# A decoder layer on one core: head values centred by TensorE, squares taken from PSUM, x2 normalised by ScalarE, the first chunk's attention prepared in the last state-space chunk

## What is computed

```python
# 1. state space: delta = softplus(x W), per step h = exp(delta*A)*h + delta*B*x, y = sum(h*C) + Dp*x, layer norm, W_out
# 2. gated attention, 4 heads of 32 columns, sequence length 64
log_D = log_fg_mat + swapaxes(ig)            # causal, gates in logarithms
D = exp(log_D - max(log_D))
C = (q k^T / sqrt(32)) * D
normalizer = maximum(abs(sum(C)), exp(-max_log_D))
h = (C / (normalizer + 1e-6)) @ v            # q = x, k = v = context
out = (h - mean(h)) * rsqrt(var(h) + 1e-5) * outnorm_scale       # per head
# 3. mixture of 8 experts, the best 2 for each token
```

## Time and profile before

| | us |
|---|---|
| median of 3 runs | 725.03 |
| lowest, highest | 715.24, 731.83 |
| the profiled execution | 720.35 |
| its span, first to last instruction | 718.5 |

### The profile page before, as it was taken

How to read it: one execution, slowest core, us unless ns; L and a number is a source line. 1 busy time by engine, 2 the same in 40 slices (tenths; PEclk the granted TensorE clock), 3 DMA queues, 4 the chain that set the end, 5 groups by cost and what they waited for, 6 DMA issues and landing times.

```text
span 718.5 us, 10709 instructions
## 1 busy us (share of the span) xinstructions
PE 535.5 (75%) x3309; PEld 378.0 (53%) x3309; DVE 447.3 (62%) x975; ACT 308.4 (43%) x628; POOL 373.4 (52%) x318
## 2 busy tenths in 40 slices
PE   3497878889788688777365779787895959999900
PEld 1032424335243335666354668676684748899900
DVE  1589999999999973379657475746361431222245
ACT  2455474856648342122132445454442413333327
POOL 1497978989788754113543354534444342333351
PEclk9999999999999988555556698999797978999955
DMA  5433435344462514463252544442434336689774
GB/s 160 148 120 139 155 133 192 125 165 155 161 189 106 205 61 89 89 99 67 57 139 44 162 150 146 149 170 92 141 126 152 110 132 201 218 284 296 252 227 132
DMA packets 87545, 106.63 MB, mean 148 GB/s; under 512 B 40912, under 2 KB 68816, under 8 KB 87360
## 3 DMA queue, kind: packets, MB, share of 16 engines
q1 hardware_dynamic: 78800, 93.08, 42.1%
q0 software_dynamic: 4320, 8.92, 3.6%
q10 hardware_dynamic: 4368, 3.93, 1.7%
HBM read 93.57 MB, written 12.34 MB: 147 GB/s over the span
## 4 chain that ended last, share of the span: by engine, by line
issue 30%; POOL 19%; PE 18%; DVE 14%; DMA 9%; ACT 4%; SPq 2%; another core or an unknown queue 1%; DVEq 0%; POOLq 0%; ACTq 0%
POOL hc L660 9%; PE pB L1058 6%; DMA wslot<-in_expert_w 5%; DVE h L1477 3%; PE pq L1071 3%; POOL xg_dram L760 3%; PE py L840 3%; POOL y_dram L769 2%; DVE u L1468 2%; ACT x_all L1430 1%; PE py L1058 1%; POOL bcs L613 1%; DMA y_dram<-dx,xin 1%; POOL bc_rest L605 1%; DMA Crep<-c_dram 1%
## 5 line engine op out<-in xcount | busy, mean ns | idle before, releaser
L660 POOL TENSOR_TENSOR hc<-h,Crep 128x1024 f32<-128x1024 f32 x64 | 150.0, 2355 | 23.7 <-DVE h L1477 22.6
L769 POOL DMA_INDIRECT y_dram<-dx,xin x71 | 68.8, 968 | 155.9 <-ACT dx L1354 146.7
L1058 PE MATMUL pB<-Crep,wslot 128*128 128x256 f32 (+1 forms) x556 | 121.7, 365 | 18.7 <-DMA wslot<-in_expert_w 10.3
L840 PE MATMUL py<-hc,ident 128*128 128x512 f32 x256 | 122.8, 608 | 4.3 <-POOL hc L660 4.3
L1058 PEld LDWEIGHTS pB<-Crep,wslot 128*128 128x128 f32 x556 | 92.7, 208 | 36.5 <-DMA wslot<-in_expert_w 13.1
L1468 DVE TENSOR_TENSOR u<-dx,pC 128x1024 f32<-128x1024 f32 x64 | 76.9, 1202 | 18.5 <-PE pC L829 18.5
L840 PEld LDWEIGHTS py<-hc,ident 128*128 128x128 f32 x256 | 49.4, 196 | 55.3 <-issue 42.1
L1791 DVE TENSOR_TENSOR Crep<-u,pB 128x512 f32<-128x512 f32 x35 | 24.0, 686 | 86.9 <-PE pB L1058 48.5
L829 PE MATMUL pC<-bcs,sel 96*128 96x512 bf16 x128 | 41.0, 403 | 45.0 <-DVE u L1468 39.8
L1477 DVE TENSOR_TENSOR_SCAN h<-pa,u 128x1024 f32<-128x1024 f32 x32 | 73.0, 2281 | 0.0
L1477 DVE TENSOR_TENSOR_SCAN h<-pB,u 128x1024 f32<-128x1024 f32 x32 | 73.0, 2281 | 0.0
(11 more groups left out here) (224 smaller groups left out, 948.2 us busy)
## 6 DMA issues: line engine op xcount, KB each, us to landing
wslot<-in_expert_w SPq DMA_DIRECT2D x46, 768.0 KB
Crep<-c_dram SPq DMA_DIRECT2D x64, 512.0 KB, 3.7
h<-m_dram SPq DMA_DIRECT2D x16, 256.0 KB
xin<-xg_dram SPq DMA_DIRECT2D x25, 130.0 KB
xbuf<-in_x_tok SPq DMA_DIRECT2D x8, 256.0 KB, 4.6
cT_st<-in_ctx_T SPq DMA_DIRECT2D x8, 256.0 KB, 4.6
dx<-in_ctx_T SPq DMA_DIRECT2D x8, 256.0 KB, 4.7
delta<-in_ctx_tok SPq DMA_DIRECT2D x32, 64.0 KB
```

The lines of the kernel that those rows point to most:

```text
L660: nc.gpsimd.tensor_tensor(hc[:, K % 4], h[:, K % 3], Crep[:, K % 4].rearrange("p a t -> p (a t)"), ALU.mult).then_inc(hc_done, 1)
L769: nc.gpsimd.indirect_dma_start(out=y2_dram, out_offset=bass.IndirectOffsetOnAxis(ap=xin[:, i % NX, a, D:D + 1].bitcast(i32), axis=0), in_= ...
L840: last = nc.tensor.matmul(py[:], ident[:], hc[:, K % 4, i * CH:(i + 1) * CH], start=False, stop=(K % STEPS == STEPS - 1 and i == 1))
L1058: last = nc.tensor.matmul(bank[:, o * a * P:(o + 1) * a * P], wslot[:, i % NW, stage * F + f * P:stage * F + (f + 1) * P], xgT[i % 2][:, 0 ...
```

## The change

- Values: TensorE multiplies the context by a 128x128 matrix `hcenter` (identity minus 1/32 within each head), so each head's values are centred before they are weighted; ScalarE copies them from PSUM (`copy_values`). The four DMAs for the values go, hsum and the centring too.
- Squares: ScalarE squares the weighted values straight from PSUM; the sum is multiplied twice by the reciprocal of the normaliser. Part 0 multiplies by outnorm out of PSUM; one factor (`vfac`) is applied in part 9.
- Gates: `add_gates` goes; the exponent becomes 16 instructions of 64 columns, each with its gate as bias, after `scale_heads` instead of before it.
- x2: part 13 makes only the shift, ScalarE normalises with four instructions.
- Logits and ranks go to pa[:,1]; `turn_x2` waits for the ranks to be read, `logits` no longer for hv.
- First chunk: its buffers are in wslot's space, so its context, maxima, mask, exponents, values and first scores stand in the last state-space chunk or right behind it; orders are changed on all engines.

```diff
+        lmask = (flatw[:, 0:W2], u[:, 0])
+        mb = (flatw[:, 0:W2], h[:, 2])
...
@@ SyncE @@
-            store_m(0)
             next_rows(NCH - 1)
-            load_m(0)
-            load_heads(0)
-            load_v(0)
+            load_heads(1)
+            load_m(1)
             next_rows(NCH)
-            load_m(1)
...
+                    if c + 1 == NCH and k == 1:
+                        load_heads(0)
+                    if c + 1 == NCH and k == 6:
+                        store_m(0)
+                    if c + 1 == NCH and k == 7:
+                        load_m(0)
...
@@ GpSimd, in the loop over the steps @@
                     weigh_state(STEPS * c + k)
+                    if c + 1 == NCH and k == 6:
+                        start_mask(0)
...
                         if c == 1:
                             mask_constants()
+                            head_constants()
...
@@ TensorE @@
+            def head_values(c):
+                pe.wait_ge(heads_loaded, 16 * (c + 1))
+                pe.wait_ge(ones_set, H + 2)
+                if c:
+                    pe.wait_ge(sq_done, c)
+                else:
+                    pe.wait_ge(u_done, STEPS * NCH)
+                for b in range(TB):
+                    last = nc.tensor.matmul(pC[:, 0, b * P:(b + 1) * P], cTc[late(c)][:, b * P:(b + 1) * P], hcenter[:],
+                                            start=True, stop=True)
+                last.then_inc(values_made, 1)
...
             def turn_x2(c):
                 pe.wait_ge(x2_done, c + 1)
                 if c:
-                    pe.wait_ge(x2T_copied, c)
+                    pe.wait_ge(ranks_read, c)
...
             sum_state(STEPS * NCH - 2)
+            head_values(0)
+            scores(0, 0)
+            scores(0, 1)
             sum_state(STEPS * NCH - 1)
             turn_m(0)
             center_y(NCH - 1)
-            scores(0, 0)
+            scores(0, 2)
+            scores(0, 3)
             variance(NCH - 1)
             turn_x1(NCH - 2)
-            scores(0, 1)
+            weighted_values(0, 0)
+            weighted_values(0, 1)
             project(NCH - 1)
             gate_products(NCH - 2)
-            scores(0, 2)
-            weighted_values(0, 0)
-            scores(0, 3)
-            weighted_values(0, 1)
...
-                expert_units(first[1:3])
+                expert_units(first[1:2])
+                if front:
+                    head_values(c + 1)
+                expert_units(first[2:3])
...
@@ ScalarE @@
             def weight_decay(c):
-                act.wait_ge(log_decay_done, c + 1)
-                if c:
+                act.wait_ge(causal_done, c + 1)
+                act.wait_ge(g_made, 1 if c < GATED[0][1] else 2)
+                if c == 1:
+                    act.wait_ge(hc_done, STEPS * NCH)
+                elif c:
                     act.wait_ge(C_done, c)
-                nc.scalar.activation(Dm, lmask, ACT.Exp).then_inc(D_done, 1)
+                for m in range(TB * H):
+                    last = nc.scalar.activation(Dm[late(c)][:, m * S:(m + 1) * S], lmask[late(c)][:, m * S:(m + 1) * S], ACT.Exp,
+                                                bias=g_sb[:, c * TB * H + m:c * TB * H + m + 1])
+                last.then_inc(D_done, 1)
...
+            def normal_x2(c):
+                act.wait_ge(x2_shift_done, c + 1)
+                act.wait_ge(z2_rstd_done, c + 1)
+                for b in range(TB):
+                    last = nc.scalar.activation(x2_rows(c)[:, b], z2[:, b], ACT.Identity, scale=rstd[:, b:b + 1],
+                                                bias=nma[:, b:b + 1])
+                last.then_inc(x2_done, 1)
...
+            weight_decay(0)
             z_scale(NCH - 2)
             copy_y(NCH - 1)
+            copy_values(0)
             normal_x1(NCH - 2)
             square_y(NCH - 1)
             y_scale(NCH - 1)
             copy_x1T(NCH - 2)
             floor_gates(0)
-            weight_decay(0)
...
+                if mid:
+                    scale_heads(c)
                 if front:
                     weight_decay(c + 1)
-                if mid:
-                    scale_heads(c)
+                    copy_values(c + 1)
                 expert_units(first[2:])
...
                 if mid:
                     z2_scale(c)
+                    normal_x2(c)
                 expert_units(second[2:])
...
@@ VectorE, order of a round @@
-                mid(0)
-                if front:
-                    add_gates(c + 1)
-                mid(1, 2, 3, 4)
+                mid(0, 1, 2)
+                rt(0)
+                mid(3, 4)
                 expert_units(first[0:1])
-                mid(5, 6)
-                rt(0)
+                mid(5, 6, 7)
                 expert_units(first[1:2])
-                mid(7)
                 rt(1)
                 if front:
                     weights(c + 1, 0)
...
-                mid(8)
+                mid(8, 9)
                 rt(7)
+                mid(10)
                 if front:
                     weights(c + 1, 1)
                 expert_units(second[0:1])
                 rt(8)
-                mid(9)
+                mid(11)
                 rt(9)
-                mid(10)
+                mid(12)
                 expert_units(second[1:2])
-                rt(10)
-                mid(11)
-                rt(11)
-                mid(12)
+                rt(10, 11)
+                mid(13)
                 rt(12, 13, 14, 15, 16)
-                expert_units(second[2:3])
-                mid(13)
-                expert_units(second[3:])
+                expert_units(second[2:])
                 rt(17, 18, 19, 20)
...
             row_stats(NCH - 2)
+            log_norm(0)
             row_means(NCH - 2)
-            log_norm(0)
-            add_gates(0)
+            weights(0, 0)
+            weights(0, 1)
             residual_rows(NCH - 1)
-            weights(0, 0)
             keep_gates(NCH - 2)
-            weights(0, 1)
```

More of the change, by code:

```diff
@@ L132, in decoder_layer @@
         norm_inv = sb("norm_inv", [P, TB * H])
-        hsum = sb("hsum", [P, TB * H])
+        vfac = sb("vfac", [P, TB * H])
+        hcenter = sb("hcenter", [P, P])
+        nma = sb("nma", [P, TB])
         vsum = sb("vsum", [P, TB * H])
@@ L374, in decoder_layer, with late @@
         CONSTS = 24
+        def late(c):
+            return int(c >= 1)
         def close_wait(engine):
@@ L467, in next_rows, with store_m, load_m, load_heads @@
                     sp.dma_start(cT_st[:], ctx_T[:, tokens(c - 1)]).then_inc(context_loaded, 16)
+            m_v = m_dram.rearrange("(c n) (j s) -> j c n s", n=TB * H, j=2)
+            def store_m(part):
+                lo, hi = (v * TB * H for v in GATED[part])
+                sp.wait_ge(m_ready, part + 1)
+                sp.dma_start(m_dram[lo:hi], mrow[lo:hi, part]).then_inc(m_stored, 16)
+            def load_m(c):
+                sp.wait_ge(m_stored, 16 * (1 if c < GATED[0][1] else 2))
+                if c == 1:
+                    sp.wait_ge(hc_done, STEPS * NCH)
+                elif c:
+                    sp.wait_ge(causal_done, c)
+                for j in range(2):
+                    sp.dma_start(mb[late(c)].rearrange("p (m s) -> p m s", s=S)[64 * j:64 * j + 64],
+                                 m_v[j, c:c + 1].broadcast_to([64, TB * H, S])).then_inc(maxima_loaded, 16)
+            def load_heads(c):
+                if c == 1:
+                    sp.wait_ge(u_done, STEPS * NCH)
+                elif c:
+                    sp.wait_ge(qk_done, H * c)
+                    sp.wait_ge(values_made, c)
+                sp.dma_start(cTc[late(c)], ctx_T[:, tokens(c)]).then_inc(heads_loaded, 16)
             store_C(0)
@@ L1588, in weights @@
                     pick = lambda v: v.rearrange("p (b h s) -> p h b s", h=H, s=S)[:, hh]
-                    last = nc.vector.scalar_tensor_tensor(pick(Cm), bank, scale, pick(Dm), ALU.mult, ALU.mult)
+                    last = nc.vector.scalar_tensor_tensor(pick(Cm[late(c)]), bank, scale, pick(Dm[late(c)]), ALU.mult, ALU.mult)
                 last.then_inc(C_done if pair else C_half, 1)
@@ L1594, in normalize @@
                 s0 = c * NSTEP
+                heads = hv.rearrange("p (m e) -> p m e", m=M)
+                lines = hv.rearrange("p (b d) -> p b d", b=TB)
                 if part == 0:
                     dve.wait_ge(av_done, c + 1)
+                    if c:
+                        dve.wait_ge(z2_done, c)
+                    else:
+                        dve.wait_ge(hc_done, STEPS * NCH)
+                    for a in range(2):
+                        half = TB // 2
+                        last = nc.vector.tensor_tensor(hv[:, a * half * D:(a + 1) * half * D].rearrange("p (b h e) -> p b h e", b=half, h=H),
+                                                       pav[:, a].rearrange("p (b h) e -> p b h e", h=H)[:, :, :, 0:HD],
```

(4 more changed lines are left out.)

200 lines of the change are left out of this document (87 added, 113 removed).

## The result

The changed kernel takes 746.58 us (median of 5 runs, 746.28 to 751.53) against 725.03 (715.24 to 731.83): 1.0358 times as long, 95% interval 1.0311 to 1.0405, slower. So the two profiles stand 31 us apart and the medians 21.5; what the traces say of places holds, their sum overstates.

What follows compares the result with a forecast made beforehand. VectorE was taken to bound rounds 1 to 3, a loop through GpSimd's sends and the queues the late rounds. Terms 1.5+1.6+10.0+5.4+3 = 21.5 us gave 742 from the profiled execution, 746 from the median; forecast 743, range 735 to 748 (chance 0.5).

Steps and rivals of the forecast that it cites:

- Two of my signs: Signs of being right: rounds 1 and 2 near 20 and 28 us; rounds 5 to 7 unchanged or 1 to 3 longer.
- Round 0: From chunk 0's first normalising instruction to chunk 1's: exponents again behind the heads' scale, +1.6 us.
- Sixteen exponents: ScalarE's exponent as sixteen 64-column instructions instead of one of 1.04 us: 3.4 us, hence +2.4, bounds 2.4 and 4.3.
- Round 1: VectorE waits for router's logits, then exponents; first `weights` at +9.9, not +5.7; less removed passes, +3.7 us.
- Round 2, +4.0, and round 3, +2.3: Same waits as round 1; round 2's logits 0.4 us later, round 3 with 2.6 on TensorE before the first expert tile.
- Second halves: Rounds 4 to 7: x2 normalised on ScalarE delays Silu, VectorE's earlier statistics give back 0.6; +1.35 us each, 5.4 together.
- TensorE's clock: Rounds 5 to 7: first halves ending earlier make longer waits, so TensorE starts at half clock; +3 us, bounds 0 and 5.
- First halves: Rounds 4 to 7: expert unit 2 to 3 us earlier, covered by GpSimd's sends and weight loads; costed at nothing.
- Transition: First chunk prepared in the last state-space chunk: `row_means` there ends 1.5 us later, bounds -4.5 and +3.
- (b): Rival, faster: VectorE's instruction count sets every round, with ScalarE's exponents beside it; -21 us, 704; chance 0.1.
- (a): Rival, slower by less: upper clock through the transition, no later clock cost, earlier logits in rounds 1 to 3; 730; chance 0.25.
- (c): Rival, slower by more: exponents take 4.3 us, rounds 5 to 7 begin second halves at 1.2 GHz; 749; chance 0.15.

Runs made afterwards that it cites:

- e1: The changed kernel with the sixteen exponents ahead of the heads' scale on ScalarE again; 736.04 us, 1.024 of the kernel before.
- e9: The changed kernel with GpSimd waiting until its first four sends of a chunk have landed; 745.26 us, 1.0323 of the kernel before.
- e5: The changed kernel with x2 made by VectorE again and part 13 back at its old place; 744.00 us, 1.0271 of the kernel before.
- e6: The changed kernel with exponents ahead of the heads' scale, logits read after the head parts and x2 by VectorE; 731.95 us, 1.0129 of the kernel before.
- e7: The kernel before with logits and ranks in the free half of the scores' banks, TensorE not waiting for head values; ratio 0.9984.
- e12: e6 with GpSimd's wait for four sends in chunks 0 and 1, TensorE held for head variances in rounds 5 and 6; 721.45 us, 1.0044 of the kernel before.
- e11: The kernel before with GpSimd waiting until its first four sends of a chunk have landed; 739.69 us, ratio 1.019.
- e8: The changed kernel with 40 very small fills on VectorE and 32 very small copies on ScalarE added; 748.04 us against 721.86 for the kernel before.
- e2: The changed kernel with VectorE's copy of the router's logits moved behind the head parts; 743.31 us, 1.030 of the kernel before.
- e3: The changed kernel with exponents ahead of the heads' scale and the logits' copy behind the head parts; 731.18 us, 1.014 of the kernel before.

## Why the prediction was right

The forecast was 743.0 us, the median is 746.58, inside the range and on the side given the most chance. The waits of rounds 0 and 1 were forecast with their causes; that the total came so near is in part luck. My terms summed to 21.5 us, the medians' difference, but the two profiled executions that the terms speak of lie 31 us apart, and single terms were off both ways. Two of my signs also failed: round 2 took 25.9 us, not near 28, and rounds 5 and 6 grew by 4.7 and 7.1 us, not by up to 3. Against the two profiled executions:

- *Round 0, +1.6*: +2.5 (19.7 to 22.2). Putting the exponents first takes 1.7 of it away (e1: 20.5), so the cause is the named one; the sixteen were 0.5 too short in my sum.
- *Sixteen exponents, 3.4 us*: 3.91 in every round; the term was mis-sized. My line through the spacings at 128 and 512 columns (0.265 and 0.61 us) gave 0.207 us at 64; measured are 0.239 between one start and the next. The Trainium skill, "ScalarE: Activation LUTs", section "What ACT_TABLE_LOAD costs", gives 280 ns plus 0.833 ns a column for an instruction with a pointer bias, less 93 ns of overlap between neighbours. An estimate by these figures is 3.94 us for the sixteen, and the trace's 3.91 agrees.
- *Round 1, +3.7*: +3.6, with the two waits where I put them: 2.73 for 2.8 and 4.34 for some 4, `weights` at +9.73 for +9.9. The wait of part 13 for ScalarE was 0.60 to 0.95 us.
- *Round 2, +4.0, and round 3, +2.3*: +1.4 and +7.1. In round 3 e9 takes 4.6 us off with a gap in the train (32.5 us), so held results, a thing that no step of mine has, can have that share. But e1 takes 6.6 us off (30.5) by ScalarE's order alone, though VectorE still waits 6.18 us there for the logits, 6.49 in the changed kernel. So the 7.1 us can't be split between the two. Why round 2 lost so little I didn't try.
- *Second halves, +1.35 a round*: +1.05 in round 6's last leg (15.10 to 16.15), where e5 and e6 (14.55) split it into 1.6 for `normal_x2` and 0.55 given back by the rest of the change. I had 1.95 and 0.6.
- *TensorE's clock, +3 over rounds 5 to 7*: round 5 has it, 1.5 us more in the middle leg and 17.50-16.15 = 1.35 in the last, which begins with matmuls of 3.35 us for 1.99: 2.9 in all, in one round; round 6 starts at the upper level.
- *First halves, costed at nothing because the sends and the weight load cover them*: as for a gain, e7 agrees. But I counted only what could be saved, and no step of mine has results of TensorE coming late within the sends. In round 6 the middle leg is 7.2 us longer (13.08 for 5.85), and e9's gap brings it back to 5.62 on the same order of instructions: that loss was missing from the sum. Whether TensorE's no longer waiting for hv is what brings it on isn't shown: e7 takes that wait alone away, has lags of up to 4.5 us and loses no time, and e12's short rounds have the rivals named above.
- *Transition, +1.5*: round 0 starts at 300.51 for 300.79, no cost. Over the eleven profiled kernels with the new transition it starts at 299.2 in the mean (297.8 to 300.5), over the three with the old one at 300.2 (299.7 to 300.8): if anything 1 us is gained. The term was 2 us too high. `row_means` behind `log_norm` wasn't tried alone.
- The end, from the last `idx` on, took 151.7 us for 148.1; over the fourteen traces it runs from 144.9 (e1) to 153.4 (e11), and no run ties the 3.6 us to a part of the change.

Against the rivals: (b), VectorE's instruction count sets every round, isn't borne out by e6, which has some 2.5 us less of VectorE a round (the 3.6 less x2's 1.1), most of round 1's waits for logits and exponents gone, and is 1.3% slower than the kernel before; its late rounds have held results, so it isn't a clean test of them. (a) was out by its number, and (c) has the better time for the exponents (3.91, a little nearer to its 4.3 than to my 3.4) and the nearer number, 749.

## What to carry to other kernels

Work taken from the engine with the highest busy share pays only if what stood behind it isn't a wait: here five passes of VectorE hid the logits and the exponents, and the removed 3.6 us came back as two waits of 2.7 and 4.3. Where one engine takes over many small instructions, place them ahead of work that waits for somebody, not behind it; that was worth all of the loss in round 1. Before crediting the removal of a wait, cut a round at the marks of its loop (here `idx`, load, first matmul) in the traces before and after, and look at the leg that grew. And when an edit seems to cure something, look also where the edit doesn't reach: e12's rounds 7 and 8 were cured as well, so its hold can't be given the credit without the kernel beside it that lacks the hold.

## What the runs showed of the hardware

In thirteen of the fourteen traces TensorE's results are handed on late during trains of GpSimd's indirect sends. The signature in the profile is a "remote" wait of VectorE and ScalarE at the same time, on things that TensorE is recorded to have begun long before: 10.05 and 9.48 us in the changed kernel, 9.06 and 9.18 in e8, and 9.20 to 9.31 on ScalarE in nine more places in rounds 5 and 6 of e1, e2, e3, e5 and e6. A gap in the train lets them out, all within 0.2 us of each other (e9). Without a gap the longest lags end with the train, as at 494.30 to 495.88 in the changed kernel, but some results come out in the middle of one: in its round 7 the logits at 533.75, in a train issued from 525.87 to 537.23.

A train alone doesn't do it: e12 has trains as long, and not one result over 0.03 us late. The kernel before stands 3.42 us in round 5 with nothing begun but the scores, and holds them 3.6 us; e12 does the same and doesn't. So the release by a gap is shown and the cause isn't: whether it is a matter of what TensorE has begun, of the chip, of the recording, whose own records go missing in the same trains, or of a resource that sends and matmuls share stays open.

Runs of one kernel lie 8 us apart (e5: 738.96 to 746.55), e8's 20 and those of the kernel before 17, so below 1% only many runs on one chip say anything; e7 and e12 had twelve each.
